# A two-layer graph network on one core: 24 chunks' part of n computed in the other half of each step, all of them in the last

## The reference

```
def step(h, _):
    messages = h[col] @ W_msg.T + b_msg
    agg = jax.ops.segment_sum(messages, row, num_segments=num_nodes)
    gi = agg @ W_ih.T + b_ih
    gh = h @ W_hh.T + b_hh
    i_r, i_z, i_n = jnp.split(gi, 3, axis=-1)
    h_r, h_z, h_n = jnp.split(gh, 3, axis=-1)
    r = jax.nn.sigmoid(i_r + h_r)
    z = jax.nn.sigmoid(i_z + h_z)
    n = jnp.tanh(i_n + r * h_n)
    h_new = (1.0 - z) * n + z * h
    return (h_new, None)
```

## Time and profile before

| | us |
|---|---|
| three runs, median (lowest to highest) | 6062.97 (6059.9 to 6068.76) |
| the profiled execution | 6070.89 |
| its span, first to last instruction | 6069.1 |
| PE, DVE, ACT, POOL busy | 3915.4, 4012.0, 2470.6, 3402.0 |

### The profile page before, as it was taken

How to read it: one execution, slowest core, us unless ns; L and a number is a source line. 1 busy time by engine, 2 the same in 40 slices (tenths; PEclk the granted TensorE clock), 3 DMA queues, 4 the chain that set the end, 5 groups by cost and what they waited for, 6 DMA issues and landing times. The chain is left out here.

```text
span 6069.1 us, 59767 instructions
## 1 busy us (share of the span) xinstructions
PE 3915.4 (65%) x13552; PEld 2135.7 (35%) x13552; DVE 4012.0 (66%) x8207; ACT 2470.6 (41%) x4771; POOL 3402.0 (56%) x3449
## 2 busy tenths in 40 slices
PE   3554545740244491000888999989999998995498
PEld 1222222310022140000665555555555544453343
DVE  5776666358766537885777766776687668663266
ACT  3664222221222131110666744664475457543333
POOL 2554777777577654776665700650073027567767
PEclk8786766875566695555999999999999999996599
DMA  5663111677411197773786633653465346663244
GB/s 219 216 226 120 45 46 46 232 253 250 143 46 46 42 311 217 205 208 103 249 259 200 200 128 130 191 175 131 141 202 159 130 157 204 193 217 109 53 131 123
DMA packets 574540, 979.61 MB, mean 161 GB/s; under 512 B 98392, under 2 KB 250862, under 8 KB 573980
## 3 DMA queue, kind: packets, MB, share of 16 engines
q1 hardware_dynamic: 459580, 761.44, 38.6%
q0 software_dynamic: 100544, 163.41, 10.0%
q10 hardware_dynamic: 14112, 51.39, 2.1%
HBM read 543.13 MB, written 438.34 MB: 162 GB/s over the span
## 5 line engine op out<-in xcount | busy, mean ns | idle before, releaser
L1630 POOL DMA_INDIRECT r_G<-msg_tab,srow x980 | 926.7, 946 | 1273.5 <-DMA msg_tab<-r_m 958.8
L855 PE MATMUL cv_psO<-cv_V,cv_cwi 128*128 128x448 f32 x896 | 473.0, 695 | 866.8 <-DVEq L841 866.8
L855 PEld LDWEIGHTS cv_psO<-cv_V,cv_cwi 128*128 128x128 f32 x896 | 217.7, 250 | 1122.1 <-issue 595.7
L1175 POOL DMA_INDIRECT x_tab<-a_r,node_pos x392 | 380.5, 971 | 232.1 <-issue 115.3
L1704 PE MATMUL r_psS<-r_sel,r_G 128*128 128x129 f32 x1960 | 326.9, 317 | 275.0 <-DMA r_G<-msg_tab,srow 157.4
L1809 DVE TENSOR_TENSOR agg<-r_psS,agg 128x129 f32 x980 | 283.3, 289 | 321.8 <-PE r_psS L1704 244.4
L721 POOL DMA_INDIRECT o_tab<-cv_ob,put_idx x392 | 388.5, 991 | 143.5 <-issue 111.6
L1673 PE MATMUL r_psHN<-r_hin,whh 128*128 128x512 f32 x882 | 458.1, 601 | 8.8 <-DMA r_hin<-ht_tab 8.7
L1678 PE MATMUL r_psR<-r_hin,whh 128*128 128x512 f32 x882 | 453.9, 596 | 0.0
L713 POOL DMA_INDIRECT cv_M<-h_tab,gat_src x392 | 374.3, 955 | 119.5 <-issue 119.5
L1662 PEld LDWEIGHTS r_psM<-wmsg,r_hnew 128*128 128x128 f32 x2744 | 349.0, 192 | 218.1 <-DVE r_hnew L1862 123.9
(11 more groups left out here) (263 smaller groups left out, 10036.2 us busy)
## 6 DMA issues: line engine op xcount, KB each, us to landing
r_hin<-ht_tab SPq DMA_DIRECT2D x441, 256.0 KB
msg_tab<-r_m SPq DMA_DIRECT2D x392, 256.0 KB
ht_tab<-r_hnew SPq DMA_DIRECT2D x343, 256.0 KB
o_tab<-o_blank SPq DMA_DIRECT2D x98, 512.0 KB, 6.4
st_h<-h_tab SPq DMA_DIRECT2D x98, 512.0 KB
st_o<-o_tab SPq DMA_DIRECT2D x98, 512.0 KB
i_x<-x_tab SPq DMA_DIRECT2D x49, 528.0 KB
r_x<-x_tab SPq DMA_DIRECT2D x98, 264.0 KB, 3.0
```

Of the source, the lines that this page charges most:

```text
L855: ins = nc.tensor.matmul(psO[:, h, 0:HW], cwi[m][:], V[i % 2][m][:, HW * h:HW * (h + 1)], start=m == 0, stop=m == 3)
L1175: pool.indirect_dma_start(x2_tab, bass.IndirectOffsetOnAxis(ap=node_pos[:, j:j + 1], axis=0), rb[i % RR][:, t, :], None).then_inc(s_out[i ...
L1630: pool.indirect_dma_start(G[g % GR][:, q, :], None, msg_tab[s % 3], bass.IndirectOffsetOnAxis(ap=srow[:, j:j + 1], axis=0)).then_inc(s_g[g ...
```

## The change

TensorE computes the states' part of n (product and bias) for some chunks of half 1 already in the gather half of the same step. In steps 0 to 3 it does so behind `tiles` of every second job (i = 1, 3, ... 47), for chunks 0 to 23; in step 4 in each of the 49 iterations, for all 49 chunks. Such a product takes a third load of SP from `ht_tab` into `r_oin`, a product into a bank of its own, `psO`, an ACT operation that adds the bias and writes `r_ohn`, and a store to a new table in DRAM, `hn_tab`. In the edge half these jobs leave out the product L1673; SP loads the kept part to `r_kin`, and DVE multiplies it with r from SBUF. For the bank, the tile sums take one bank instead of two, and are 128 columns wide instead of 129.

```
--- before.py
+++ after.py
-SW = P + 1
+SW = P
...
+        AHEAD = [(s, i, i // 2) for s in range(FIN1) for i in range(1, HALF, 2)] + [(FIN1, i, i) for i in range(HALF)]
...
+            psO = pb("r_psO", [P, CW], F32, c6)
...
-            psS = [pb(f"r_psS{i}", [P, 2, 256], F32, c6) for i in range(2)]
+            psS = pb("r_psS", [P, TQ, SW], F32, c6)
...
+                def load_ahead(a):
+                    s, _, c = AHEAD[a]
...
+                    if a >= 2:
+                        sp.wait_ge(s_op, a - 1)
+                    sp.dma_start(oin[a % 2][:], htv[HALF + c]).then_inc(s_oin[a % 2], 16)
+
+                def store_ahead(a):
+                    sp.wait_ge(s_oe, a + 1)
+                    sp.dma_start(hnv[AHEAD[a][2]], ohn[a % 2][:]).then_inc(s_ost[a % 2], 16)
+
+                def load_kept(k):
+                    s, h, i = JOBS[k]
+                    a = ahead_of[s, i]
+                    sp.wait_ge(s_ost[a % 2], 16 * (a // 2 + 1))
+                    if k >= 2:
+                        sp.wait_ge(s_t1, k - 1)
+                    sp.dma_start(kin[k % 2][:], hnv[i]).then_inc(s_kin[k % 2], 16)
...
                     sp.wait_ge(s_d1, k + 1)
                     if k + 2 < len(JOBS):
                         load(k + 2)
+                        if kept(k + 2) and (JOBS[k + 2][0] < FIN1 or JOBS[k + 2][2] >= 2):
+                            load_kept(k + 2)
+                    if h == 0 and i % 2 == 0:
+                        if i == 0:
+                            load_ahead(ahead_at[s, 1])
+                        else:
+                            store_ahead(ahead_at[s, i - 1])
+                        if i + 3 < HALF:
+                            load_ahead(ahead_at[s, i + 3])
...
+                def ahead(a):
+                    pe.wait_ge(s_oin[a % 2], 16 * (a // 2 + 1))
+                    if a:
+                        pe.wait_ge(s_oe, a)
+                    nc.tensor.matmul(psO[:], whh[:, 2 * D:3 * D], oin[a % 2][:], start=True, stop=True
+                                     ).then_inc(s_op, 1)
...
                         if i >= 2:
                             tiles(HALF * s + i - 2)
+                        if (s, i) in ahead_at:
+                            ahead(ahead_at[s, i])
...
-                        hidden(k)
+                        if kept(k):
+                            pe.wait_ge(s_hin[k % 2], 16 * (k // 2 + 1))
+                        else:
+                            hidden(k)
...
                         if i:
                             select(HALF * s + i - 1)
+                        if (s, i) in ahead_at:
+                            a = ahead_at[s, i]
+                            act.wait_ge(s_op, a + 1)
+                            if a >= 2:
+                                act.wait_ge(s_ost[a % 2], 16 * (a // 2))
+                            nc.scalar.activation(ohn[a % 2][:], psO[:], ACT.Identity, bias=bhh[:, 2:3]).then_inc(s_oe, 1)
...
-                    nc.vector.scalar_tensor_tensor(ts[k % 2][:], psHN[k % 2][:], bhh[:, 2:3], rs[k % 2][:],
-                                                   ALU.add, ALU.mult).then_inc(s_t1, 1)
+                    if kept(k):
+                        nc.vector.tensor_tensor(ts[k % 2][:], kin[k % 2][:], rs[k % 2][:], ALU.mult).then_inc(s_t1, 1)
+                    else:
+                        nc.vector.scalar_tensor_tensor(ts[k % 2][:], psHN[k % 2][:], bhh[:, 2:3], rs[k % 2][:],
+                                                       ALU.add, ALU.mult).then_inc(s_t1, 1)
```

More of the change, by code:

```diff
@@ L172, in build @@
     ht_tab = dram("ht_tab", (D, NPAD))
+    hn_tab = dram("hn_tab", (D, EPAD))
     msg_tab = [dram(f"msg{i}_tab", (NPAD, D)) for i in range(3)]
@@ L1505, in build, with kept @@
             x2_n.append(n[2])
+        AHEAD = [(s, i, i // 2) for s in range(FIN1) for i in range(1, HALF, 2)] + [(FIN1, i, i) for i in range(HALF)]
+        ahead_at = {(s, i): a for a, (s, i, _) in enumerate(AHEAD)}
+        ahead_of = {(s, c): a for a, (s, _, c) in enumerate(AHEAD)}
+        own_n, kept_n, n = [], [], [0, 0, 0]
+        for k, (s, h, i) in enumerate(JOBS):
+            kept = h and (s, i) in ahead_of
+            n[2] += not kept
+            n[k % 2] += bool(kept)
+            own_n.append(n[2])
+            kept_n.append(n[k % 2])
+        def kept(k):
+            s, h, i = JOBS[k]
+            return bool(h) and (s, i) in ahead_of
         def job(s, h, i):
@@ L1534, in build @@
         s_fin = [stage_sem("r_fin0"), stage_sem("r_fin1")]
+        s_oin = [stage_sem("r_oin0"), stage_sem("r_oin1")]
+        s_ost = [stage_sem("r_ost0"), stage_sem("r_ost1")]
+        s_kin = [stage_sem("r_kin0"), stage_sem("r_kin1")]
+        s_op, s_oe = stage_sem("r_op"), stage_sem("r_oe")
         c6 = ExitStack()
@@ L1550, in build @@
             stg = [sb(f"r_stage{i}", [P, TPC, D], F32, c6) for i in range(3)]
+            oin = [sb(f"r_oin{i}", [P, CW], F32, c6) for i in range(2)]
+            ohn = [sb(f"r_ohn{i}", [P, CW], F32, c6) for i in range(2)]
+            kin = [sb(f"r_kin{i}", [P, CW], F32, c6) for i in range(2)]
             psHN = [pb(f"r_psHN{i}", [P, CW], F32, c6) for i in range(2)]
+            psO = pb("r_psO", [P, CW], F32, c6)
             psR = pb("r_psR", [P, CW], F32, c6)
@@ L1591, in staged @@
                     sp.dma_start(stg[i % 3][:].rearrange("p t f -> p (t f)"), msgv[2][i]).then_inc(s_sg[i % 3], 16)
+                def load_ahead(a):
+                    s, _, c = AHEAD[a]
+                    if s:
+                        b = job(s - 1, 1, c)
+                        sp.wait_ge(s_hst[b % 2], 16 * hst_n[b])
+                    if a >= 2:
[5 more added lines that the diff above has]
+                def load_kept(k):
+                    s, h, i = JOBS[k]
+                    a = ahead_of[s, i]
[3 more added lines that the diff above has]
+                    sp.dma_start(kin[k % 2][:], hnv[i]).then_inc(s_kin[k % 2], 16)
                 load(0)
@@ L1598, in _ @@
                         store_m(k - 1)
+                    if turn and s == FIN1:
+                        for j in range(HALF + 1):
+                            if j == 0:
+                                load_ahead(ahead_at[s, 0])
+                                load_ahead(ahead_at[s, 1])
+                            elif j + 1 < HALF:
+                                load_ahead(ahead_at[s, j + 1])
+                            if j:
+                                store_ahead(ahead_at[s, j - 1])
+                        load_kept(k)
+                        load_kept(k + 1)
                     sp.wait_ge(s_d1, k + 1)
@@ L1613, in _ @@
                 for par in range(2):
+                    sp.wait_ge(s_ost[par], 16 * ((len(AHEAD) + 1 - par) // 2))
                     sp.wait_ge(s_hst[par], 16 * count[par][0])
@@ L1828, in hidden @@
                     s, h, i = JOBS[k]
-                    dve.wait_ge(s_hn, k + 1)
+                    if kept(k):
+                        dve.wait_ge(s_kin[k % 2], 16 * kept_n[k])
+                    else:
+                        dve.wait_ge(s_hn, own_n[k])
                     dve.wait_ge(s_r, k + 1)
```

6 lines of the change are left out of this document (4 added, 2 removed).

## The result

The changed kernel takes 6080.94 us (median of 20 runs, 6070.73 to 6099.31), the kernel before 6068.23 (20 runs). The ratio is 1.0020, 95% interval 1.0013 to 1.0027: 8 to 16 us slower, some 12.7 by the medians. The forecast was 6065 in a range of 6050 to 6086, with +1.6 us as the sum of the change; the time lies in the range, and the sum was some 10 us too low. The profiled execution has a span of 6079.8 us against 6069.1. Every ratio here compares fast runs alone while the times are medians of all runs, and on the chip of the first four experiments many runs were slow, so there the two don't match.

The account below looks back on a forecast made before the run. Bounds: a dependence loop in gather halves of steps 0 to 3, PE in edge halves, POOL in the last step. 80.0 - 82.4 + 5 + 1 - 2 = +1.6 us; forecast 6065 us, range 6050 to 6086.

Parts of the forecast that it names:

- The gather half: Steps 0 to 3: 93 added products behind `tiles`, 0.86 us each, lengthen the gather halves by 80.0 us.
- The loop: Gather halves: `tiles`, `psHN`, PE's product of r, ACT's r, DVE's adds, next `tiles` form a closed 5.26 us period.
- the prediction's first rival: Gather halves: the added product fits PE's 0.96 us idle per job, gaining 82 us, about 5985; chance 0.05.
- The edge half: Steps 0 to 3: removed products save 0.86 us each, period 5.18, -82.4 us in all; step 3 returns +5.
- The rival that wanted 15 there: Step 3's edge half +15 from late loads at period 5.8, last edge half +13; 6086, chance 0.25.
- The step that failed: Edge halves, steps 0 to 3: without job 0's product the second `tiles` comes some 0.8 us earlier at most.
- The last step: Step 4: gather half absorbs 49 products at 0; last edge half stays set by POOL's stores; about +1 us.
- The holding of 0.47 a job: Last edge half: DVE operations with two SBUF inputs delay POOL's four stores by 0.47 us, period 5.63.
- rival of a half that runs free: Last edge half: no POOL store held, period 5.16 instead of 5.63, 23 us less, 6042; chance 0.08.
- Tile sums: Sums 128 wide instead of 129 save 0.01 us in some 196 periods: -2 us.
- two large terms that nearly cancel: Steps 0 to 3: +80.0 us for products added to gather halves, -82.4 us for those removed from edge halves.

Follow-up runs that it names:

- the first four experiments: Changed kernel with product between z and messages, only last step, chunks 1 to 24, or r in PSUM: 6710.8, 6725.6, 6662.1, 6678.2 us; before there 6740.8.

## Why the prediction was right, and where its sum was off

**The gather half: right.** The loop was read from one period, and the price and the place were both confirmed: +77.1 for +80, and 79 us back in the whole when the product is moved into the gap. The gap is 0.82 us of a period, 5.26 less the 4.44 of PE's own work by the distances of its starts, and not the 0.96 of the prediction's first rival. That changes nothing, since 0.86 in a gap of 0.82 gives the 5.30 measured. **The edge half: right**, 19.7 a step in steps 0 to 2 for the 19.8 worked out, period 5.18. In step 3 it gained 17.0, 2.8 us less than in the other steps, where 5 was allowed; the DMA engines ran at 0.92 of their time at 296 GB/s, forecast 97%. The rival that wanted 15 there had the price too high.

**The step that failed: job 0 of the edge half.** The prediction said that without its product the second `tiles` "comes some 0.8 earlier at most", and took this in full: four times -0.8, -3.3 in all. It measured +5.8. This term is 9.1 us off, as much as the sum of the traces (10.7 against 1.6), while the errors of the other rows, up to 2.9 each, cancel. Two things were wrong. First, the product isn't on the turn's chain: the second sum starts 4.38 us after the first with the product or without, in 50 of 52 turns, since DVE has a job's update, a move of messages and four adds to do in between. So there was nothing to gain there. Second, the clock was taken as given, but the row at 3503.11 already has 1.73 us where a sum takes 1.13: it was at half there. Before the change it was at half in the four turns for 3.4, 6.8, 6.8 and 3.4 us, after it for 10.2, 6.8, 6.8 and 13.7. The product, useless to the chain, kept PE busy between two sums; without it PE idles 1.76 us more and its sums on the chain run at 1.2 GHz instead of 2.4. That the missing product is the cause is supported by the 22 of 36 turns with at most 3.4 us at half clock against none of 16. What the length of a turn depends on is where in it the clock is low; why the clock falls at one place in one turn and at another in the next stays open.

**The last step: right in its result.** The gather half took the 49 products for +0.7. The last half did not follow PE from 5.59 to 4.73, nor DVE to 4.95, but kept POOL's pace: most jobs of DVE take 5.0 us and then some wait up to 2.7 for a landing, and a job takes 5.58 to 5.59 on average in both kernels. By the stores' own time after has 276.1 us over 49 jobs, 5.63, the number forecast; but by the same measure before has 5.61, not 5.59. The holding of 0.47 a job was worked out from chances and measured 0.44. That it is held stores and not something else that sets the half was argued ahead and is now shown. The prediction's rival of a half that runs free did not come, but r and n in PSUM produce just that: 256.7 us in 49 jobs is 5.24, near its floor of 5.16. Of the Trainium skill, SBUF, section "Who interferes with whom", both halves of the rule held here: a VectorE instruction with two inputs in SBUF kept POOL's store waiting (1.41 us), the same with one of them in PSUM did not (0.98).

**Tile sums: -2 forecast, 0 measured.** The prediction took the sum's shorter time as a gain of the loop. Three of four gather halves with the narrower sums differ by 0.2 us or less from before.

So the forecast of no change was right because two large terms that nearly cancel were right to 3 us each. The rest is in part luck: the 12.7 us between the medians lie at the very limit of the 12 us that the prediction called no change, and the small terms, of the size of what a measurement tells, decided the side. Of the 16 us between the forecast of 6065 and the measured 6080.9, 5 come from the base, since the three runs of before that were shown had a median of 6063.0 and the twenty have 6068.2.

## What to carry over

In a closed loop of dependences a step costs nothing or its whole length depending on its place: find the gap ahead of the wait and put the added work there (here 79 us by moving one product). Before taking work out of an engine that idles nearby, look whether its clock in that stretch is at the edge of falling; work that the chain doesn't need can keep it up. And when one engine is relieved in a half in which three are nearly full, price the next two before hoping: 49 products removed from a full PE gave 0 until the stores of POOL were freed, and then the half fell from 267.7 to 248.0 us in the traces.

## What the runs showed of the hardware

- POOL's indirect store out of SBUF is held by an operation of DVE with both inputs in SBUF that is under way when it starts. Over the 392 stores of this form in the trace of before, duration = 0.985 us + (shown end of DVE's operation - 0.12 - start) with a mean error of 3.5 ns, and 0.985 alone where there is no such operation (this says how long a store takes, not what in it waits). In all 13 traces together, 1416 stores started inside such an operation, more than 0.16 us ahead of its end, and 1345 of them follow this within 0.03 us. Of the 1305 that started as far ahead of the end of an operation with one input in PSUM none took more than 1.02 us.
- Who starts first matters. The other 71 of the 1416 started in the first 0.045 us of DVE's operation. None of them was held (at most 0.99 us), and it was DVE's operation that became longer, 0.72 to 0.77 us instead of 0.68 to 0.70.
- POOL's indirect gathers (L1630) took 0.94 to 1.00 us in all traces, but none of them ever started inside an operation of DVE with both inputs in SBUF, so whether a gather would be held is not shown.
- PE's granted clock falls to half within the turns although PE is busy 12 of 16 us there, and with a product less it stayed down for 10.2 or 13.7 us instead of 3.4 in two of four turns.
- The DMA engines at 0.92 of their time (296 GB/s) let a period of some 5.3 us pass in step 3's edge half of after: 2.8 us less gain than in the other steps. Asked for more, with 48 chunks, that half took 256.4 us where those of the other steps took 248.9.
